# The macaron block's schedule rewritten: key sums carried by VectorE, the feed-forwards' input product in four runs, and another order of work on all four engines

## The reference: what is computed

```python
x = x + 0.5 * ffn(layernorm(x))
x = x + attn(layernorm(x))
x = x + 0.5 * ffn(layernorm(x))

# ffn, both times with the same weights (64 hidden groups of 16 units)
s = layernorm(x) @ Win + bin_                    # 512 -> 64
h = relu(s[..., None] * W1 + b1)                 # 16 units each
g = sum(h * W2, axis=-1) + b2                    # 64
out = g @ Wout + bout                            # 64 -> 512

# attn: causal linear attention, 16 heads of 32
q, k, v = split(x @ w_attn)                      # 512 -> 3 x 512
q, k = elu(q) + 1, elu(k) + 1
S = S + outer(k_t, v_t);  z = z + k_t            # running state of a sequence
y_t = (q_t @ S) / (sum(q_t * z) + 1e-6)
attn = y @ w_proj
```

## Time and profile before

| what | value |
|---|---|
| median of three runs | 2559.25 us (2556.72 to 2559.64) |
| the profiled execution | 2556.46 us |
| its span, first to last instruction | 2554.7 us |
| mean granted TensorE clock | 0.983 of full speed |
| busy: PE, DVE, ACT, POOL | 93%, 74%, 56%, 34% of the span |
| matmul rows of PE | 33282 |

### The profile page before, as it was taken

One profiled execution on the slowest core, in us unless ns is written; L12 is line 12 of the kernel. 1 busy time (PEld: TensorE's weight loads), 2 busy tenths in 40 slices (PEclk: granted clock), 3 DMA queues, 4 the chain that ended last, 5 costly groups with the idle time before them and its releaser, 6 DMA issues.

```text
span 2554.7 us, 75807 instructions
## 1 busy us (share of the span) xinstructions
PE 2373.4 (93%) x33282; PEld 1799.6 (70%) x33282; DVE 1892.7 (74%) x3248; ACT 1422.0 (56%) x2248; POOL 867.4 (34%) x996
## 2 busy tenths in 40 slices
PE   2799999999999999999999999999999999999995
PEld 1577777777777777777777777777777777777773
DVE  4578777778777778777777877777877777877755
ACT  3456565556565555556555656555656555556544
POOL 4332333333333333233333233333333333323221
PEclk8899999999999999999999999999999999999997
DMA  5000011001011111001110001111100111000000
GB/s 161 1 2 25 12 35 35 35 35 35 2 35 35 35 35 35 18 19 35 35 35 35 35 2 35 35 35 35 35 3 34 35 35 35 35 18 2 18 18 34
DMA packets 39355, 76.97 MB, mean 30 GB/s; under 512 B 4081, under 2 KB 4081, under 8 KB 39026
## 3 DMA queue, kind: packets, MB, share of 16 engines
q1 hardware_dynamic: 39026, 72.12, 8.2%
HBM read 38.56 MB, written 33.55 MB: 28 GB/s over the span
## 4 chain that ended last, share of the span: by engine, by line
PE 86%; DVE 5%; ACT 4%; issue 3%; SPq 0%; POOL 0%; DMA 0%; DVEq 0%; POOLq 0%
PE bank L916 31%; PE att L916 27%; PE att L934 6%; PE att L1010 6%; PE att L1035 4%; PE att L944 3%; DVE yl L632 3%; ACT yh L390 2%; PE att L1026 2%; PE bank L951 2%; PE att L981 1%; PE att L968 1%; PE bank L944 1%; DVE acc_psum L650 1%; ACT v L390 1%
## 5 line engine op out<-in xcount | busy, mean ns | idle before, releaser
L413 ACT ACTIVATE xhat<-res,nmr,rstd 128x512 f32<-128x512 f32 x384 | 303.0, 806 | 324.2 <-DVE nmr L623 297.0
L432 ACT ACTIVATE ffr<-ffs,b1c,w1c 128x512 f32<-128x512 f32 (+1 forms) x544 | 430.6, 810 | 17.5 <-DVE acc_psum L650 7.9
L650 DVE SCALAR_TENSOR_TENSOR acc_psum<-ffr,w2c,acc_psum 128x512 f32<-128x512 f32 (+1 forms) x476 | 354.4, 745 | 49.4 <-ACT ffr L432 34.2
L326 POOL TENSOR_SCALAR_AFFINE_SELECT A<-A 128x512 f32<-128x512 f32 x256 | 158.7, 637 | 683.7 <-ACT A L390 683.7
L314 POOL TENSOR_TENSOR res<-res,hbout 128x512 f32<-128x512 f32 x256 | 325.1, 1288 | 127.6 <-ACT xhat L413 127.6
L616 DVE BATCH_NORM_STATS2 st<-res 128x6 f32<-128x512 f32 x384 | 261.7, 682 | 17.1 <-DMA res<-in_L_attn_x_dram 8.8
L916 PE MATMUL att<-xh,wa_h 128*128 128x512 f32 x560 | 228.8, 408 | 15.4 <-DVE xl L632 15.4
L390 ACT ACTIVATE A<-att 128x512 f32<-128x512 f32 x256 | 142.5, 596 | 145.8 <-PE att L1010 143.4
L916 PE MATMUL att<-xl,wa_h 128*128 128x512 f32 x560 | 221.9, 396 | 0.0
L916 PE MATMUL att<-xh,wa_l 128*128 128x512 f32 x560 | 221.8, 396 | 0.0
L702 DVE TENSOR_TENSOR A<-att,tri 128x512 f32<-128x512 f32 x256 | 171.9, 683 | 57.2 <-PE att L1010 57.1
(11 more groups left out here) (112 smaller groups left out, 5649.3 us busy)
## 6 DMA issues: line engine op xcount, KB each, us to landing
res<-in_L_attn_x_dram SPq DMA_DIRECT2D x32, 1024.0 KB, 5.3
out_dram<-res SPq DMA_DIRECT2D x32, 1024.0 KB, 4.3
kT<-in_L_attn_w_attn_dram SPq DMA_DIRECT2D x1, 1024.0 KB, 5.4
qT<-in_L_attn_w_attn_dram SPq DMA_DIRECT2D x1, 1024.0 KB, 7.6
v<-in_L_attn_w_attn_dram SPq DMA_DIRECT2D x1, 1024.0 KB, 10.7
A<-in_L_attn_w_proj_dram SPq DMA_DIRECT2D x4, 256.0 KB, 11.6
win<-in_L_ffn_Win_dram SPq DMA_DIRECT2D x4, 128.0 KB, 6.1
wo<-in_L_ffn_Wout_dram SPq DMA_DIRECT2D x2, 128.0 KB, 4.6
```

What stands on the lines that cost most here:

```text
L326: eng.affine_select(out=A[:, h, :, :], in_=A[:, h, :, :], compare_op=ALU.is_ge, fill=0.0, base=0, pattern=[[0, 4], [1, P]], channel_multip ...
L413: eng.activation(xhat[t % 2][:, :], res[b % SLOTS][:, t, :], ACT.Identity, bias=nmr[:, n, t:t + 1], scale=rstd[:, n, t:t + 1]).then_inc(s_ ...
L432: eng.activation(ffr[i % 2][p, :], ffs[p, :], ACT.Relu, bias=b1c[p, i:i + 1], scale=w1c[p, i:i + 1]).then_inc(s_hr, 1)
L650: eng.scalar_tensor_tensor((ffs if i == INNER - 1 else psum)[p, :], r[p, :], w2c[p, i:i + 1], psum[p, :], ALU.mult, ALU.add).then_inc(s_hm, 1)
```

## The change

Four things are changed at once.

1. The copy `zc` of the running sum's last column moves from POOL to DVE (`carry`), and is made for even blocks only, since no block continues an odd one.
2. `ff_in` is cut into four runs (`PARTS`), each over four of the sixteen channel groups. `values(j, 0, 0)` stands between the first two runs, `values(j, 0, 1)` between the second and the third; the third and the fourth follow each other.
3. The order of the calls is another one on PE, ACT, DVE and POOL.
4. The order in which products are given PSUM banks follows PE's new order.

```diff
+PARTS = 4
...
+        def carries(b):
+            return b % PER < PER - 1
+        def carried(b, g):
+            return 4 * (b // PER * (PER - 1) + b % PER) + g + 1
...
 (POOL, zsum)
-                eng.tensor_copy(zc[:, g:g + 1], z[:, BLK - 1:BLK]).then_inc(s_zc, 1)
-                e.wait_ge(s_zc, 4 * b + g + 1)
+                if carries(b):
+                    e.wait_ge(s_zc, carried(b, g))
                 eng.tensor_tensor(z, qT[:, g, :], z, ALU.mult).then_inc(s_zq, 1)
...
 (DVE)
+            def carry(b, g):
+                e.wait_ge(s_scan, 4 * b + g + 1)
+                eng.tensor_copy(zc[:, g:g + 1], z2[:, g % 2, BLK - 1:BLK]).then_inc(s_zc, 1)
...
 (PE)
-            def ff_in(j):
-                take_all("in", j, 0)
+            def ff_in(j, part):
+                if part == 0:
+                    take_all("in", j, 0)
...
-                for c in range(C // D):
+                n_c = C // D // PARTS
+                for c in range(n_c * part, n_c * part + n_c):
...
-                op.then_inc(s_fi, 1)
+                if part == PARTS - 1:
+                    op.then_inc(s_fi, 1)
```

More of the change, by code:

```diff
@@ L559, in _ @@
                 if on(j - 1) or on(j + 2):
+                    hidden(j, 8)
                     hidden(j, 9)
-                if on(j + 1):
-                    channels(j + 1, 0)
+                if on(j):
+                    score(j, 0, 2)
+                    score(j, 0, 0)
+                if on(j - 1) or on(j + 2):
+                    hidden(j, 10)
                 if on(j):
@@ L565, in _ @@
                     ysplit(j, 0)
+                    key(j, 2)
+                if on(j + 1):
+                    channels(j + 1, 0)
+                if on(j - 1) or on(j + 2):
+                    hidden(j, 11)
                 if on(j + 1):
                     normalise(L2, j + 1, 2)
-                    channels(j + 1, 1)
-                    normalise(L2, j + 1, 3)
                 if on(j):
@@ L572, in _ @@
                     score(j, 1, 2)
-                    key(j, 2)
-                if on(j + 1):
-                    channels(j + 1, 2)
                 if on(j - 1) or on(j + 2):
-                    hidden(j, 10)
-                    hidden(j, 11)
+                    hidden(j, 12)
                 if on(j):
@@ L751, in _ @@
                     transposed(1, j + 2, 0)
+                if on(j):
+                    zsum(j, 0)
+                if on(j) and carries(j):
+                    carry(j, 0)
+                if on(j + 2):
                     transposed(1, j + 2, 1)
@@ L1062, in _ @@
             eng.matmul(o[:, :], tri[0:1, :], z2[0:1, 1, :], start=True, stop=True).then_inc(s_mbout, 1)
-            ff_in(-1)
+            for part in range(PARTS):
+                ff_in(-1, part)
             for b in range(2):
@@ L1101, in _ @@
                 if on(j):
-                    attend(j, 0)
-                    update(j, 0)
+                    update(j, 1)
+                    scores(j, 1)
+                    outer(j, 0, 0)
                 if on(j + 1):
@@ L1106, in _ @@
                 if on(j):
-                    key(j, 2)
-                    scores(j, 1)
+                    attend(j, 1)
+                    outer(j, 0, 1)
                 if on(j + 1):
@@ L1111, in _ @@
                 if on(j):
-                    outer(j, 0, 0)
+                    scores(j, 2)
+                    update(j, 2)
+                    outer(j, 1, 0)
+                    attend(j, 2)
+                    outer(j, 1, 1)
+                if on(j + 2):
+                    ff_out(1, j + 2, 0, j)
+                    ff_out(1, j + 2, 1, j)
+                if on(j):
+                    scores(j, 3)
+                    outer(j, 2, 0)
+                    key(j, 3)
+                    attend(j, 3)
                 if on(j + 1):
@@ L1138, in _ @@
                 if on(j - 1):
+                    ff_out(0, j - 1, 0, j)
                     ff_out(0, j - 1, 1, j)
```

308 lines of the change are left out of this document (152 added, 156 removed).

## The result

The changed kernel takes 2523.97 us (median of four runs, 2523.58 to 2526.51) where the kernel before takes 2559.02: a ratio of 0.9867, 95% interval 0.985 to 0.9884, estimated from all runs of both (the two medians alone give 0.9863). By the medians that is 35 us faster, where 23 were forecast, well inside the range. All rows of the changed kernel are from its profiled execution, 2526.51 us with a span of 2524.7.

A forecast was written before the change was run, and what follows sets the result against it. PE, busy 2373.4 of 2554.7 us, was taken to bound the kernel; the terms sum to -0.75 us an iteration, -23 us in 31 iterations, from 2556.5 to 2533.5, forecast as 2536 us for the median, with a range of 2489 to 2566.

The forecast's parts named there:

- standstill in `ff_in`: PE's idle time in the long `ff_in` run, read as instruction supply running dry, nearly goes: -1.1 us an iteration.
- two seams: Two more changes on PE between three-part and small float32 products and back, 0.20 us each: +0.4 us an iteration.
- wait before `scores(3)`: PE's wait for `yl` before `scores` of tile 3 goes, covered by half of `outer(1)` and two `ff_out`: -0.55 us.
- wait before `spread`: PE's wait for the copy of v before `spread` goes, with nothing left by a hair only: -0.45 us an iteration.
- wait before the last `outer`: PE's loss behind `yl` of tile 3 goes, filled by `channels` and half of `outer(2)`: -0.75 us in the mean.
- halves of `ff_out`: `ff_out` passes on the same 64 partitions run one after another, four more deep: +1.7 us an iteration, bounds 0.8 and 1.7.
- carry: Moving the copies from POOL to DVE, where they lie ahead of hidden 0 to 2: taken as 0.
- under the shortest that broke, 188: The longest `ff_in` run without anything slower, 128 rows, was held safe because the shortest run seen to break had 188.
- the rival of the gap: Idle time in `ff_in` stays (+0.35 us an iteration, 2570), or half stays or returns as small waits (2553); chance 0.15.
- The free passes: Rival: the extra `ff_out` passes lie under other work and cost nothing: -2.45 us an iteration, 2483 us; chance 0.12.
- The late chain: Rival: DVE's hidden 0 to 15 takes 37.4 us again, the first `ff_out` is 3.4 late: +2.65, 2641 us; chance 0.13.
- 4 us of room: DVE's work from hidden 0 to hidden 15, 29.8 us, fits the 34 us before the first `ff_out`, with 4 over.

The follow-up runs named there:

- the run with 192 and 64: The changed kernel with `ff_out` halves alternating, and `ff_in` cut into runs of 192 and 64 matmul rows instead of four runs: 2492.53 us, ratio 0.9757.
- the first experiment: The changed kernel with the two `ff_out` ahead of `scores(3)` one of each half and the last six alternating: 2486.23 us, ratio 0.9725.
- the second: The changed kernel with `ff_in` in one run again and both halves of `values(j, 0)` behind it: 2544.65 us, ratio 0.9951.
- the run with two spares: The changed kernel with two extra VectorE statistics operations, result unused, ahead of hidden 13: 2550.58 us, ratio 0.9988.
- the run with two pieces of 128: The changed kernel with `ff_out` halves alternating, and `ff_in` in two runs of 128 rows, both halves of `values(j, 0)` between: 2471.87 us, ratio 0.968.
- with four: The changed kernel with four extra VectorE statistics operations, result unused, ahead of hidden 13: 2669.54 us, ratio 1.0434.

## Why the prediction was right, point by point

**The sum.** Forecast -0.75 us an iteration, measured -0.93. By terms:

| term | forecast | measured | from |
|---|---|---|---|
| standstill in `ff_in` | -1.1 | -1.6 | mean step before 5.36 us, without a break 0.26 + 4 x 0.88 = 3.78 |
| two seams | +0.4 | +0.9 | two runs against four |
| wait before `scores(3)` | -0.55 | -0.55 | wait gone |
| wait before `spread` | -0.45 | -0.45 | 0.5 us left in the whole program |
| wait before the last `outer` | -0.75 | -0.75 | no wait on `yl` left there |
| halves of `ff_out` | +1.7 | +1.56 | starts, with the halves as they are and alternating |
| carry | 0 | 0 | with and without, in both orders |

The measured column sums to -0.89. A term that I had put at 0 is missing in it: PE's new wait behind POOL's mask, 4.5 us in all, 0.15 an iteration. With it 0.19 us of the 0.93 is not assigned by these terms. A second account closes. In both traces I added up the distances from each matmul's start to the next over iterations 2 to 29, by kind of product. The changed kernel has -1.05 us an iteration at `ff_in`, +0.40 at the projections and v, -1.54 at `key` (where the waits before `scores` and `spread` lie), +0.44 at the two products of `attend` (0.13 of it POOL's wait), +0.81 at `ff_out` and `outer` together and -0.03 at the rest: -0.97, as the iterations themselves (75.78 to 74.82). So the two waits gave more than the 1.00 us that their listed idle time says, and `attend` took most of it back; why it did is open. The three waits in the middle are read from the two traces, and each by itself was not tested; what isolates them together is the run with one `ff_in` again, order and carry without the cut: 75.38 us, 0.39 less than before, although the halves cost 1.56 in it. Its `ff_in` accounts for 0.2 of that, since it did not break every time.

**Where it was off.** Two terms were mis-sized by 0.5 us each, and that their errors cancel is luck. I had left 0.3 us of idle time in `ff_in`, and nothing was left; and I had taken a row's time as 15.4 ns, which is wrong. The 3.34 us of the 217 rows reach to the end of the last one, and rows overlap. In the page's group the second number behind the bar is the mean duration of one row, 281 ns:

```profile
L934 PE MATMUL att<-xf,win 32*64 32x128 f32 x8192 | 149.8, 281 | 61.5 <-issue 41.0
```

(3.34 - 0.28) / 216 is 14.2 ns from start to start, about what unbroken runs have (0.88 us for 64, 13.8 ns). So all 256 rows want under 3.8 us, not 3.94, and I saw only 1.4 of the 1.6 us. And I had taken a seam at the 0.20 that a product of twelve matmuls loses between float32 neighbours, but `ff_in` loses 0.26 of its own at each cut as well. A smaller error is the 0.14 of `ff_out`. The mechanisms were right, with two readings to be corrected below. The sum was made against the profiled execution: there it was -23 by forecast and 2526.51 - 2556.46 = -30 by measurement; 29 x 0.93 = 27 is the loop's. The other 5 of the 35 us are where medians lie beside the profiled executions.

**The instruction supply.** The prediction read two iterations and had the run break at no fixed matmul, after 188 rows at the earliest. Over all iterations the breaks of the kernel before come after 131 to 246 rows. Two of the early ones in its timeline of PE:

```profile
788.41 2.20 PE L934 MATMUL att<-xf,win 32*64 32x128 f32 x132
791.56 2.06 PE L934 MATMUL att<-xf,win 32*64 32x128 f32 x124 [0.96 <-issue]
...
1470.03 2.15 PE L934 MATMUL att<-xf,win 32*64 32x128 f32 x131
1473.58 2.06 PE L934 MATMUL att<-xf,win 32*64 32x128 f32 x125 [1.41 <-issue]
```

And they do have a fixed place, in the stream of instructions and not in the run. I numbered all of PE's records in the order of their starts: matmuls, weight loads and those of its sequencer. The number at which a break comes, divided by 256, leaves 193 or 194 in every one of the 28 breaks that the kernel before has in iterations 2 to 29 (34.0 us of idle time). The same holds for the 28 breaks with the carry alone, the 24 in the run with one `ff_in` and the 13 in the run with 192 and 64. The instructions come in pieces of just that size. In the page of the kernel before, a queue of its own carries them:

```profile
q8 instruction: 263, 4.31, 0.7%
```

263 packets of 16384 bytes stand against 67372 records of PE, one packet for 256. And after each of the 28 breaks PE goes on between 1.26 and 1.53 us after the end of the latest of these packets. So PE stands still at the edge of a block that has not come.

This also says when a run breaks. A row has a weight load beside it, so 128 rows are one block and a run of 256 crosses two edges. The first edge never broke a run, the second did in all of iterations 2 to 29. In iteration 1 it did not, and there the lower clock, shown with the result, let most rows start at about half the pace:

```profile
183.05 5.68 PE L934 MATMUL att<-xf,win 32*64 32x128 f32 x256 [2.12 <-issue]
```

Of the 29 runs of 192 in iterations 1 to 29, 16 cross a second edge, of which 13 broke; of the 13 others none did. A run of 128 rows is as long as one block. Hence my limit for it, "under the shortest that broke, 188", was a wrong reading of the trace (the shortest had 131), and that four parts gave a longest run of just one block is luck. The argument against the rival of the gap, that "the break comes after different counts", does not hold either: the counts within the run differ, the places in the stream do not. What remains of it is the pace, since the runs that broke are fast ones with a second edge. Not shown is how far ahead PE asks for a block, and why 3 of the 16 runs, and 5 of 29 with one `ff_in`, came through; in all of these the second edge lay at row 133 to 148.

The rule of the Trainium skill (Runtime: NRT & Kernel Launch, Instruction fetch mechanics) that fetching is mostly hidden does not fit this stretch: the 34.0 us of idle time were lost at the edges of blocks.

**The rivals.** The free passes fell with the first experiment, the gap that stays with the second. The late chain did not come by itself. In the iteration that starts at 1221.81 hidden 0 begins 26.2 us in (26 forecast) and the first `ff_out` 59.7 us in (60 forecast). In the changed kernel hidden 15 starts at 1280.07 and ends at 1280.81 in the timeline of VectorE, and the first `ff_out` stands at 1281.52. Last comes the window from hidden 0 to the end of hidden 15:

```profile
1248.02 0.79 DVE L658 TENSOR_SCALAR acc_psum<-ffr,w2c,b2c 128x512 f32<-128x512 f32 x1
...
1280.07 0.74 DVE L661 SCALAR_TENSOR_TENSOR ffs<-ffr,w2c,acc_psum 128x512 f32<-128x512 f32 x1
...
1281.52 1.98 PE L972 MATMUL bank<-wo,ffs 64*128 64x512 f32 x4
```

```profile
1248.02:1280.81 32.79, 32.73 (x535) 25.27 (x534) 27.83 (x47) 25.97 (x42) 12.07 (x13) 1.00 0.01 2
```

A margin of 0.7 us, where I had found 4 us of room. That step was wrong, though it did not enter the sum: I added up VectorE's work and compared it with the window. The work was even less than I had added up, 27.8 us instead of 29.8 in a window of 33.5, but the list also waits in it for PE's `scores`, for ACT's copies and for `den`. These waits are 5.0 of the 5.7 us of room, idle time that could not be used. That the chain was still in time is in part luck. What the rival had a late chain cost, its lateness and no more, was right for a small delay (the run with two spares lost about its wait), and beyond it I had not counted the clock.

**The signs.** Iterations of about 75.0 us (74.86), no idle time before `scores` of tile 3 and `spread`, 1.91 and 3.62 us for the two groups of `ff_out`, hidden 15 in time: these came as listed. One did not to the letter: a piece of "issue" over 0.5 us is left, the 2.5 us of the first `ff_in` of the program.

## What to carry to other kernels

Before two operations on disjoint halves of the array are reordered, count the passes per half: adjacent ones of different halves are free, of the same half they add up, and an engine that is "busy" hides that. A long run of small matmuls is best cut, but only as far as needed: here two runs of 128 rows, each as long as one block of 256 instructions, beat four, since each seam costs. A wait that comes at different matmuls may still have a fixed place: number the whole stream of instructions before calling it irregular. And a static order with no slack should be judged by the margin of its latest producer, read at the place, and not by sums of work.

## What the runs showed of the hardware

A standstill costs more than its length when the granted clock falls behind it. With 0.69 us of waiting an iteration (1.4 us of extra work ahead of hidden 13) an iteration grew by 0.76 us; with 2.15 us it grew by 4.69, and the granted clock was 0.50 in windows behind two of the waits shown and 1.00 behind the third, while PE was busy throughout. Length alone does not decide: in the run with two pieces of 128, PE stood still for 2.38 us ahead of the `ff_in` at 186.62, and the granted clock is 1.00 from 186.62 to 193.00. Its mean over the span was 0.983 with two spares and 0.953 with four.

PE's instructions come in packets of 16384 bytes, one for 256 of its records. At the upper clock, rows of 32x64 weights and 128 columns start every 14 ns with a weight load each, so 128 rows use up a packet in 1.8 us. All 28 runs of 256 such rows stood still at their second edge, and no run of 128 did behind the first `ff_in` of the program.
